# Third buffers for the split keys and values, routing work packed early, shares and targets moved into the attention, key and query stores with the partition outermost

## The reference, cut to what matters

```python
def _L0_ffn_ref(x, gate_w, gate_b, w1, w2):          # E = 32 experts, K = 8 tokens each
    logits = jnp.einsum('bsd,ed->bse', x, gate_w) + gate_b
    probs = jax.nn.softmax(logits, axis=-2)           # over the tokens
    vals_t, idx_t = jax.lax.top_k(probs.transpose(0, 2, 1), K)
    ...
    tok = jnp.take_along_axis(x, flat_idx[:, :, None], axis=1)
    merged = jnp.einsum('bked,bke->bed', tok, vals)   # one merged row per expert
    h = gelu(concat[merged, 1] @ w1); o = concat[h, 1] @ w2
    out = zeros_like(x).at[arange(b)[:, None], flat_idx].add(o * vals)
# layer 0
xn = _layernorm(x)
s = attention(xn)        # q, k, v through rank-128 projections, rotary parts added to q and k
x = x + s * _silu(_L0_ffn_ref(xn, ...))
# layer 1: selective scan over d_state 16, and a SwiGLU layer, again x + s * silu(ffn)
```

## Time and profile before

| | us |
|---|---|
| median of 3 runs (2972.17 to 2976.72) | 2973.69 |
| the profiled execution | 2973.5 |
| its span, first to last instruction | 2971.8 |
| part A, from the start to the first PE work of the rounds | 82.8 |
| part B, to the end of DVE's values of round 15 | 240.1 |
| from there to the end of the stage | 42.9 |
| start of the attention to the first weighing | 30.6 |
| rest of the attention | 563.6 |
| scatter stage | 51.0 |
| layer 1 | 1960.8 |

### The profile page before, as it was taken

The page is one execution under the profiler, slowest core; times in us unless marked ns, Lnnn a source line. Parts: engine busy times, 40 slices in busy tenths (PEclk is TensorE's granted clock), DMA queues, the critical chain, the costliest instruction groups (busy, mean ns, idle before and its releaser), DMA issues. The chain is left out here.

```text
span 2971.8 us, 39206 instructions
## 1 busy us (share of the span) xinstructions
PE 2569.5 (86%) x13290; PEld 1485.8 (50%) x13290; DVE 2307.5 (78%) x2777; ACT 2025.9 (68%) x3268; POOL 2068.6 (70%) x650
## 2 busy tenths in 40 slices
PE   5876288888887669999999999999999999999977
PEld 2333133333333435665655655656656556566455
DVE  6576476656562359899899898998998998989985
ACT  3221145556565369788798888897887988888864
POOL 0454441000000159999999999999999999999996
PEclk9998579999899779999999999999999999999989
DMA  8334398767650232132231320321322313213210
GB/s 274 102 105 126 102 264 205 199 165 197 169 166 10 93 121 96 40 122 77 74 122 44 107 112 25 122 100 49 122 72 79 122 37 114 102 35 121 93 51 8
DMA packets 133884, 322.69 MB, mean 109 GB/s; under 512 B 13233, under 2 KB 89009, under 8 KB 117314
## 3 DMA queue, kind: packets, MB, share of 16 engines
q1 hardware_dynamic: 113186, 248.84, 27.4%
q0 software_dynamic: 19200, 70.73, 7.2%
q10 hardware_dynamic: 1312, 0.66, 0.1%
HBM read 277.12 MB, written 43.13 MB: 108 GB/s over the span
## 5 line engine op out<-in xcount | busy, mean ns | idle before, releaser
L1449 DVE TENSOR_TENSOR_SCAN l_st<-l_p_a,l_hl,l_st 128x512 f32<-128x512 f32 x768 | 932.5, 1266 | 106.1 <-ACT l_p_a L1708 95.2
L1630 POOL TENSOR_TENSOR l_st<-l_st,l_cs 128x2048 f32<-128x2048 f32 x192 | 871.5, 4567 | 0.0
L1708 ACT ACTIVATE l_p_a<-l_dt,lw_a_neg 128x512 f32<-128x512 f32 x1024 | 664.8, 680 | 45.2 <-DVE keep_xg L1449 37.0
L1622 POOL TENSOR_TENSOR l_st<-l_bs,l_dtu 128x2048 f32<-128x2048 f32 x128 | 584.4, 4566 | 29.7 <-PE l_p_y L1979 27.5
L1979 PEld LDWEIGHTS l_p_y<-keep_ident,l_st 128*128 128x128 f32 x3072 | 354.1, 144 | 143.7 <-POOL l_st L1630 77.0
L1979 PE MATMUL l_p_y<-keep_ident,l_st 128*128 128x128 f32 x3072 | 384.3, 281 | 48.0 <-POOL l_st L1630 47.8
L969 ACT ACTIVATE a_pr<-a_p_s 128x512 f32<-128x512 f32 x512 | 284.5, 596 | 161.6 <-PE a_p_s L1035 143.7
L893 DVE TENSOR_REDUCE a_mpart<-a_p_m 128x1 f32<-128x512 f32 x512 | 315.2, 683 | 97.7 <-PE a_p_m L1000 95.8
L1449 DVE TENSOR_TENSOR_SCAN keep_xg<-l_p_a,l_hl,keep_xg 128x512 f32<-128x512 f32 x256 | 314.8, 1267 | 1.6
L1630 POOL TENSOR_TENSOR keep_xg<-keep_xg,l_cs 128x2048 f32<-128x2048 f32 x64 | 292.5, 4570 | 2.0 <-ACT l_hl L1713 2.0
L1035 PE MATMUL a_p_s<-a_qst,kx 99*128 99x256 bf16 x1024 | 204.2, 289 | 74.1 <-ACT a_pr L969 55.1
(11 more groups left out here) (225 smaller groups left out, 3920.7 us busy)
## 6 DMA issues: line engine op xcount, KB each, us to landing
a_w<-in_w_dram POOLq DMA_DIRECT2D x64, 1024.0 KB, 11.9
l_bs<-s_bc SPq DMA_DIRECT2D x64, 1024.0 KB, 4.7
l_cs<-s_bc SPq DMA_DIRECT2D x64, 1024.0 KB, 4.8
keep_share<-s_x SPq DMA_DIRECT2D x32, 512.0 KB, 4.9
s_kp<-t_kp SPq DMA_DIRECT2D x96, 128.0 KB
kx<-s_kp SPq DMA_DIRECT2D x16, 768.0 KB, 11.1
s_vp<-t_vo SPq DMA_DIRECT2D x16, 544.0 KB
a_vg<-s_vp SPq DMA_DIRECT2D x16, 544.0 KB, 11.9
```

Source lines behind the costliest of these rows:

```text
L1449: eng.tensor_tensor_scan(st[k % NG][:, n, :], p_a[:, n, :], st[k % NG][:, n, :], hl[:, k, n:n + 1], ALU.mult, ALU.add).then_inc(scan_ok, 1)
L1622: eng.tensor_tensor(st[n][:, :, :], bs[:, 4 * n:4 * n + 4, :], dtu[(k // NG) % 2][:, :].unsqueeze(1).broadcast_to([P, NG, TT]), ALU.mult). ...
L1630: eng.tensor_tensor(st[n][:, :, :], st[n][:, :, :], cs[:, 4 * n:4 * n + 4, :], ALU.mult).then_inc(cm_ok, 1)
L1708: eng.activation(p_a[:, n, :], dt[c % 2][:, :], ACT.Exp, scale=a_neg[:, c, m:m + 1]).then_inc(dA_ok, 1)
```

## The change

- **Stores.** `kp` and `vo` get three buffers each, cut from one tensor `late` that the attention later uses for w2; `k32` gets two. The scratch tensors for keys and queries are laid out so that the outermost dimension of every store is 32 (a pair of partition group and head) where it was 4. The stage's end no longer waits for the last key and value stores: the semaphores `stored` live on, and the attention waits for them (`all_stored`) before the first load that needs them.
- **x1.** The 16 stores of x from the tile buffers go. In the attention, SP issues eight copies of 1 MB from x to `x1`, one in every second step.
- **Routing.** The pieces move to earlier rounds: row statistics at round 2 (was 3), norm 3, merge 4, the eight queries in rounds 6 to 8 (were 9 to 12), turning 8 and 9 (were 11 and 13), query splits at 10 to 12. POOL issues the eight gathers of x before `key_low` and `key_rest` of round 1, and the table rows four at a time after rounds 4 and 6. ACT's `low` of the next round comes ahead of `high`.
- **Queries.** SP stores the first part at its round 13, ACT the others after its rounds 13 and 14, and SP reads the queries of two head groups back (`group_queries`) before it stores the keys of round 15.
- **Attention.** DVE gets `one_choice` in each of 16 steps, between the maxima and `take`: half of the steps do one pick's share, half its rank, on two halves of 512 columns. The ones come from HBM, the identity's cast goes to ACT, and PE waits for the setup only at the first transpose. `eo` becomes a part of `hraw`.
- **Scatter.** `keep_xg` is overwritten in the attention, so POOL gathers the picked rows again at the start of the scatter stage.

```diff
@@ prepare_stage, SP @@
-                        eng.wait_ge(x_out[t % 4], t // 4 * 16)
...
-                    eng.wait_ge(x_in[t % 4], t // 4 * 16 + 16)
-                    eng.dma_start(scr["x1"][t * TT:(t + 1) * TT, :].rearrange("(a p) d -> p a d", p=P), xb[t % 4]).then_inc(x_out[t % 4], 16)
...
-                    p = r % 2
+                    p = r % 3
                     eng.wait_ge(kp_ok, r + 1)
                     for g in range(6):
-                        part, eo = divmod(g, 2)
-                        dst = scr["kp"][r * HG * 48:(r + 1) * HG * 48, :].rearrange(
-                            "(a q z) t -> a q (z t)", a=HG, q=6)[:, g, :].rearrange("a (z t) -> a z t", t=TT)
-                        eng.dma_start(dst, kp[p][:, part, eo, :]).then_inc(stored[p], 16)
+                        eng.dma_start(scr["kp"].rearrange("(r c a e) (h t) -> r c e a h t", c=3, a=HG * 8, e=2, h=4)[r, g // 2, g % 2],
+                                      kp[p][:, g // 2, g % 2, :]).then_inc(stored[p], 16)
...
-                for p in two:
-                    eng.wait_ge(stored[p], STORES * (NT // 2))
...
+                eng.wait_ge(side, 16 * (1 + 2 * 7 + 2 * 6))
@@ prepare_stage, DVE @@
-                    wait(eng, r1_ok, t)
+                    wait(eng, r1_ok, t - 1)
...
-                    wait(eng, stored[p], t // 2 * STORES)
+                    wait(eng, stored[p], t // 3 * STORES)
@@ prepare_stage, POOL @@
                 for t in range(NT):
                     key_rotation(t)
-                    if t:
-                        key_low(t - 1)
-                    key_rest(t)
                     if t == 1:
                         eng.wait_ge(picked, GLOBAL)
                         for k in range(K8):
                             eng.indirect_dma_start(xg[:, k, :], None, ins["x"],
                                                    bass.IndirectOffsetOnAxis(g8[:, k:k + 1], 0)).then_inc(xg_in, 16)
...
+                    if t:
+                        key_low(t - 1)
+                    key_rest(t)
@@ attention_stage, SP @@
+                    if hg % 2:
+                        half = bass.ds(b * S + hg // 2 * (S // 2), S // 2)
+                        eng.dma_start(scr["x1"][half, :].rearrange("(p a) d -> p (a d)", p=P),
+                                      ins["x"][half, :].rearrange("(p a) d -> p (a d)", p=P)).then_inc(x1_out, 16)
@@ attention_stage, POOL @@
-                for h in range(HG):
-                    eng.memset(kst[h][R:RM, :, :, :], 1.0).then_inc(ones_ok, 1)
@@ attention_stage, DVE @@
-                eng.tensor_copy(identb[:, :], ident[:, :]).then_inc(setup, 1)
+                def one_choice(g, b, hg):
+                    k = b * 2 + hg // 2
+                    wait(eng, shares, 6 * g)
+                    eng.tensor_copy(col[:, 0:1], gf[:, bass.ds(k, 1)])
+                    eng.tensor_copy(col[:, 1:2], vals[:, bass.ds(k, 1)]).then_inc(shares, 1)
+                    for h in two:
...
+                        if hg % 2 == 0:
+                            eng.tensor_scalar(found[:, :], rowb[:, cols], col[:, 0:1], col[:, 1:2], ALU.is_equal, ALU.mult).then_inc(shares, 1)
...
+                            eng.tensor_tensor(share[:, cols], share[:, cols], found[:, :], ALU.add).then_inc(shares, 1)
+                        else:
+                            eng.scalar_tensor_tensor(found[:, :], rowb[:, cols], col[:, 0:1], rankb[:, cols], ALU.is_equal, ALU.mult)\
...
+                            eng.tensor_reduce(part[:, h:h + 1], found[:, :], AX.X, ALU.max).then_inc(shares, 1)
...
+                    one_choice(*prev(g, b, hg))
+                    take(*prev(g, b, hg))
@@ scatter_stage, POOL @@
+                for k in range(K8):
+                    eng.indirect_dma_start(xg[:, k, :], None, ins["x"], bass.IndirectOffsetOnAxis(g8[:, k:k + 1], 0)).then_inc(xg_in, 16)
```

More of the change, by code:

```diff
@@ L38 @@
 EPS = 1e-5
+STORES = 16 * 7
 ATT = 1.0 / float((16 + 128 + 128) ** 0.5)
@@ L131, in prepare_stage @@
         kst = [kx[h + 1][0:96, :].bitcast(BF16).rearrange("p (c z t) -> p c z t", c=NC, z=4) for h in two]
+        ones = [kx[h + 1][96:99, :].bitcast(I32) for h in two]
         xb = [(qs, qr)[j // 2][:, 4 * (j % 2):4 * (j % 2) + 4, :] for j in range(4)]
@@ L153, in prepare_stage @@
         x_in = [sem(f"x_in{j}") for j in range(4)]
-        x_out = [sem(f"x_out{j}") for j in range(4)]
         lg_out = [sem(f"lg_out{p}") for p in two]
-        stored = [sem(f"stored{p}") for p in two]
         ones_set, eps_set = sem("ones_set"), sem("eps_set")
@@ L794, in attention_stage @@
         w1 = sb("w1", [P, 4, KD, HID])
-        w2 = sb("w2", [P, 4, 8, D])
+        w2 = late[:, :].rearrange("p (j c d) -> p j c d", j=4, c=8)
+        rowb, rankb = (keep["xg"][:, 4 * i:4 * i + 4, :].rearrange("p k d -> p (k d)") for i in range(2))
+        found = sb("found", [P, TT])
+        part = sb("part", [P, 2])
+        rank, top, dup = (sb(n, [P, TOPK]) for n in ("rank", "top", "dup"))
+        col = sb("col", [P, 2])
         b1 = sb("b1", [P, NE, 8])
@@ L830, in prev, with all_stored @@
             return (g - 1, b if hg else b - 1, (hg - 1) % HG)
+        def all_stored(eng):
+            for j in range(3):
+                eng.wait_ge(stored[j], (6, 5, 5)[j] * STORES)
         def early(b, hg):
@@ L928, in step, with last @@
                         i.then_inc(hT_ok, 1)
-                    if not (isinstance(g, int) and g == 0):
-                        take(*prev(g, b, hg))
-                passes(eng, step, lambda: take(G - 1, B - 1, HG - 1))
+                    if isinstance(g, int) and g == 0:
+                        return
+                    one_choice(*prev(g, b, hg))
+                    take(*prev(g, b, hg))
+                def last():
+                    one_choice(G - 1, B - 1, HG - 1)
+                    place()
+                    take(G - 1, B - 1, HG - 1)
+                passes(eng, step, last)
             @block.scalar
             def _(eng):
+                eng.activation(identb[:, :], ident[:, :], ACT.Copy).then_inc(setup, 1)
                 def negT(g, b, hg):
```

360 lines of the change are left out of this document (181 added, 179 removed).

## The result

The changed kernel took 2920.8 us (median of 4 runs, 2917.5 to 2928.5) against 2974.7 for the kernel before on the same chip. The ratio is 0.982, 95% interval [0.980, 0.985]: faster by 54 us or 1.8%, where 91 were forecast and 2857 was the low and 2914 the high end of the range.

The account below looks back on a forecast made before the run. Attention bound by PE, part B by waits for stores landing on a quarter of the DMA engines. -61 - 8 - 23 - 6 + 4 + 3 = -91 on 2973.5 gives 2883 us, range 2865 to 2903, with rivals 2857 to 2914.

Parts of the forecast that it names:

- part A: Preparation's first part: fewer SP store transfers and no waits for their landing shorten DVE's wait for x; -8 (0 to -16).
- part B: Preparation's second part: waits for store landings go and PE becomes the bound, 179 us against 240.1; -61 (-90 to -40).
- tail: From DVE's last values to the stage's end: 42.9 us falls to 19.5, no landing awaited; -23 (-14 to -28).
- start of the attention: Attention's first 30.6 us: the identity's cast and POOL's memsets leave DVE's way; -6.
- attention: Sixteen choices on DVE: eight covered, eight delay the next step 2 us; copies and w1, w2 waits free; +4 (0 to +16).
- scatter: Scatter stage's start: the gathers run again and hold DVE's first addition; +3 (0 to +8).
- gathers' stall: Part B, rounds 1 to 3: eight gathers hold POOL 10 us and delay PE; +8 (0 to 15).
- turned queries: Part B: DVE's two halves of them behind rounds 8 and 9, some 6 us each; +5 in all (0 to 8).
- Rival 2: Stores stay on a quarter of the engines, 10.8 us a round, tail 20 us longer: about 2913 us; chance 7%.
- Rival 1: Part B: packing costs more than the rounds had room for, 25 us more: 2908 us; chance 14%.
- Rival 4: Slower than before: the choice between bias and take makes DVE late every attention step; 2991 us at 7 us each; chance 3%.
- what would show it: Signs listed beforehand; the last wrong sign: PE waiting for w1, w2 or keys in the attention, meaning the copies aren't free.

Follow-up runs that it names:

- e1: Changed kernel with the three small loads that the choices read issued in the attention's first pass, not its last: 2894.0 us, ratio 0.973.
- e11: The changed kernel itself measured once more, without an edit: 2917.9 us, ratio 0.982 to the kernel before.
- e2: On top of e1, the choice put ahead of the hidden layer's bias in quad steps (those with experts): 2885.5 us, ratio 0.970.
- e3: On top of e1, all 16 choices put behind the last take: 2944.2 us, ratio 0.990.
- e8: On top of e2 with first queries' loads ahead of round 14's stores: gathers back behind round 0's last part and round 1's remainder; ratio 0.973.
- e5: On top of e2, key and query stores back to an outermost dimension of 4, three buffers kept: 2927.3 us, ratio 0.983.
- e4: On top of e1, each of the eight 1 MB copies of x issued twice: 2898.4 us, ratio 0.974.

## Why the prediction was right and wrong

| step | forecast | measured (profiled executions) |
|---|---|---|
| part A | -8 | -6.0 |
| part B | -61 | -55.3 |
| tail | -23 | -19.8 |
| start of the attention | -6 | -7.1 |
| attention | +4 | +28 first pair, +14 steps |
| scatter | +3 | +1.6 |
| layer 1 | 0 | -0.8 |
| sum | -91 | -45 on the span |

**The step that failed** is the attention's, and in it the last sentence: "Waits for w1 and w2 are issued a half pair ahead: 0." I priced the loads that were there and not the one wait that the change adds, on `consts` in front of the first bias. Queued behind it on DVE are the bias, `take` and the next maxima, and PE's next scores wait for them. The window of the first 30.6 us already showed the DMA engines at 0.92. What I did not see is that a small load issued last into such a queue is late twice, nor that w1 and w2 go out ahead of hg 3's key loads once POOL's memsets are gone. e1 shows the first: with the load of `rank` 30 transfers earlier in SP's queue the 28 us (23 in e11) are gone, and nothing takes their place.

**The size of the choices** was the second miss: the steps grew by 14 us, or 11 in the second measurement, where 4 were forecast; 8 of them are the choices' (e2, e3). Their duration (forecast 2.5 to 3.5 us) was nearly right, 2.9 and 3.65, and so was that eight steps cover them. Too hopeful was that PE's four banks of scores would absorb the others: the intervals ending at quad takes grew by 2.1 to 3.3 us each, almost the whole choice, and only a third of it (6.5 of 20.5 us; half in the second measurement) came back in the others. DVE's mean of 57% said nothing about that point. The range (0 to +16) held it. Its place alone made the cost, since 9 us of idle DVE lay one instruction earlier (e2).

**Part B** came out as derived, 184.8 us for 179: PE-bound, at the clock 0.94 (0.95 assumed), without waits for landings. Of the extra terms the gathers' stall is there: PE stood 7.8 us at 115.83 for ACT's `low` (8 forecast), and e8 shows that it isn't had back by that order. For the turned queries PE stood 5.34 us ahead of 191.29 and 4.76 ahead of 208.53, 10 us where 5 were forecast. Each time two of DVE's operations for them last 2.6 us and not 0.68. DVE's and POOL's timelines of the first time in the changed kernel:

```profile
183.09 2.61 DVE L398 TENSOR_TENSOR t_lg<-keep_accT,kx 128x512 f32<-128x512 f32 x1
185.62 2.60 DVE L397 TENSOR_TENSOR t_lg<-keep_accT,kx 128x512 f32<-128x512 f32 x1
188.15 0.68 DVE L398 TENSOR_TENSOR t_lg<-keep_accT,kx 128x512 f32<-128x512 f32 x1
```
```profile
182.57 2.58 POOL L565 TENSOR_TENSOR late<-t_rest,late 128x1024 bf16<-128x1024 f32 x1
185.11 2.57 POOL L571 TENSOR_TENSOR t_rest<-t_k,late 128x1024 f32<-128x1024 f32 x1
```

Each slow one of DVE runs beside one of POOL and ends 0.5 us after it, and the third, with POOL idle, takes 0.68. Against the sum, these waits cost 5 us more, PE's own work 4 more (162.0 for 158), and the rest, merge and hand-overs, 3 less: together the 5.8 by which part B missed.

**The tail**: 23.1 for 19.5. "No landing of them is waited for" holds, but an issue can be slow too: one of the three blocks of six key issues took 7.68 us for 3.8, while ACT stored queries and the DMA share was 0.90.

**Part A and the attention's start** are right in mechanism and within 2 us in size.

**The rivals.** None of the four was what happened. Rival 2 (stores stay on a quarter) had the nearest time (2913), by luck: the share of 0.56 excludes it, and taking the layout back costs 42 us (e5). Rival 1 (2908) had another cause. Rival 4 named the right place, the choice between bias and take, and far too high a price. The true loss, a new wait for a load, came closest to the last sentence of "what would show it", which speaks of a wait of PE for w1, w2 or keys.

**Still open**: why the second six key loads need 19.89 us to be issued. In the kernel before, the whole group of SP's loads at the attention's start is issued in 17 us, with three larger key loads a group. Six loads of 256 KB in the place of three larger ones, the 8 MB of w1 and w2 that now go out ahead of them (285 to 292, where the kernel before issued them after all of SP's), and one more 1 MB copy are all possible; only the copies were varied (e4), and they are not it. The few microseconds of the steps that are neither choices nor copies are open as well.

## What to carry to other kernels

When a change adds a wait, price that wait first: find in the trace where in its queue the load is issued, what is issued ahead of it, and how full the DMA engines are then; here a load of 4 KB behind megabytes landed with them. Move small loads to the front of the queue. Put added work on an engine directly ahead of the wait it already has, not behind it: the same choice was free in one place and 8 us over the loop in the other. And test a layout and a buffer apart before calling one of them enough, since here each covered a part of the other's stall.

## What the runs showed of the hardware

- The time to issue a DMA is not constant. Six key stores take SP 3.77 us on a free queue and 7.68 us at a share of 0.90; six key loads of 256 KB took 3.26 us and, seven microseconds later, 19.89.
- A 4 KB load needed 33.2 us to land when issued behind those, and 11.1 us when issued 30 transfers earlier.
- From 207 to 221 us in the changed kernel, six key loads and the stores beside them fill the DMA engines (1.03) at only 159 GB/s, while from 322 to 328 us, when weight blocks land, 394 to 405 GB/s pass in slices that are as full (in the row of slices above). A full share does not say how many bytes flow.

```profile
207.00:221.00 14.00, 12.47 (x33) 7.09 (x34) 6.97 (x14) 5.94 (x12) 6.35 (x4) 0.76 1.03 159
```
